# All edge sums beside the sort, marks made on chip, and the search for first edges inside the first node chain of a four-layer graph network

## What is computed

```python
# layer 0: weights summed per node; x scaled, a two-layer MLP, residual, layernorm
geo_sum = segment_sum(edge_weight1 * x[dst], dst); geo_agg = x + geo_sum / segment_sum(edge_weight1, dst)
x = layernorm(x + relu(relu(geo_agg @ W1 + b1) @ W2 + b2))
# layer 1: sum, max and mean of edge_attr_64 per dst node, then an MLP over the node
agg_sum, agg_max = segment_sum(edge_attr_64, dst), segment_max(edge_attr_64, dst)
h = concat([x, agg_sum, agg_max, agg_mean, u]); x = layernorm(x + layernorm(gelu(h @ W1 + b1) @ W2 + b2) + x)
# layer 2: an MLP with a gate on every edge from x[src], x[dst]; mean per SRC node
# layer 3: attention over the edges of each dst node, softmax, sum, batchnorm, gelu
```

## Time and profile before

| | us |
|---|---|
| median of three runs (range) | 6424.94 (6419.04 to 6425.12) |
| profiled execution: its span, first to last instruction | 6445.0 |
| sorted keys are there (end of the split, L545) | 824.4 |
| first load of the node chain (L1013) | 1207.4 |
| last scatter of the node chain ends | 1462 |

### The profile page before, as it was taken

How to read it: one execution, slowest core, us unless ns; L and a number is a source line. 1 busy time by engine, 2 the same in 40 slices (tenths; PEclk the granted TensorE clock), 3 DMA queues, 4 the chain that set the end, 5 groups by cost and what they waited for, 6 DMA issues and landing times. The chain is left out here.

```text
span 6445.0 us, 56951 instructions
## 1 busy us (share of the span) xinstructions
PE 3469.2 (54%) x12150; PEld 1967.8 (31%) x12150; DVE 3716.2 (58%) x4303; ACT 1751.8 (27%) x3305; POOL 3538.9 (55%) x3662
## 2 busy tenths in 40 slices
PE   3565655573443344344444424677666766776772
PEld 2344433341222222222222212333333333333331
DVE  9988955552333333333333343777777777777776
ACT  1233323371111111111111111333333333333331
POOL 5430033326666666666666656666666666666653
PEclk8566667785666666666666655767777677667665
DMA  8756457713333334333333312333333333333331
GB/s 198 208 187 202 150 154 194 132 28 91 102 103 101 103 100 106 99 101 104 106 99 100 104 43 63 86 85 87 85 87 85 86 86 85 86 86 85 88 81 32
DMA packets 994791, 677.97 MB, mean 105 GB/s; under 512 B 645273, under 2 KB 798667, under 8 KB 993734
## 3 DMA queue, kind: packets, MB, share of 16 engines
q1 hardware_dynamic: 718424, 341.42, 21.1%
q0 software_dynamic: 116880, 124.33, 10.4%
q10 hardware_dynamic: 159390, 211.24, 9.7%
HBM read 344.06 MB, written 332.55 MB: 105 GB/s over the span
## 5 line engine op out<-in xcount | busy, mean ns | idle before, releaser
L1655 POOL DMA_INDIRECT got<-tabg,ix x1568 | 1481.5, 945 | 874.7 <-DMA t<-rows 427.9
L1461 POOL DMA_INDIRECT got<-tabg,ix x1568 | 1481.5, 945 | 788.2 <-issue 455.3
L182 PE MATMUL p_out<-ident,run 128*128 128x128 f32 (+1 forms) x3136 | 667.6, 360 | 410.4 <-ACT rows L1519 213.4
L1559 DVE TENSOR_TENSOR_SCAN own<-mk,own,p_first 128x512 f32<-128x512 bf16 x195 | 247.1, 1267 | 1100.0 <-remote 874.4
L182 PEld LDWEIGHTS p_out<-ident,run 128*128 128x128 f32 (+1 forms) x3136 | 547.3, 216 | 733.4 <-issue 599.5
L1481 PE MATMUL p_inter<-hid,W 128*128 128x512 f32 x392 | 313.5, 894 | 806.3 <-issue 676.9
L1790 DVE TENSOR_TENSOR_SCAN top<-p_reset,top,logit 128x512 f32<-128x512 f32 x195 | 249.6, 1280 | 537.3 <-ACT logit L1764 228.7
L168 PE MATMUL p_small<-ident,ea 128*32 128x128 f32 (+1 forms) x784 | 179.6, 376 | 690.7 <-ACT rows L1753 613.8
L1483 PE MATMUL p_gate<-hid,WF 128*128 128x512 f32 x392 | 293.3, 841 | 285.8 <-ACT gate L1513 148.1
L1528 ACT ACTIVATE hid<-pre,B 128x512 f32<-128x512 f32 x196 | 141.2, 720 | 1113.7 <-DVE pre L1575 797.2
L498 DVE TENSOR_TENSOR_SCAN run<-p_mk,run,feat 128x512 f32<-128x512 f32 x302 | 370.5, 1268 | 54.7 <-remote 32.8
(11 more groups left out here) (348 smaller groups left out, 6831.8 us busy)
## 6 DMA issues: line engine op xcount, KB each, us to landing
t<-rows ACTq DMA_DIRECT2D x195, 512.0 KB
first<-start SPq DMA_DIRECT2D x390, 256.0 KB
t<-rows ACTq DMA_DIRECT2D x195, 288.0 KB
got<-tabg,ix POOLq DMA_INDIRECT x3136
start<-zeros SPq DMA_DIRECT2D x100, 500.0 KB
ea<-in_ea_dram SPq DMA_DIRECT2D x390, 128.0 KB
mk<-marks SPq DMA_DIRECT2D x780, 64.0 KB
start<-zeros SPq DMA_DIRECT2D x195, 256.0 KB
```

The costliest lines, as they stand in the source:

```text
L182: mm = nc.tensor.transpose(bank[0:g.p, cc, :], by_place(t, g)[:, :, cc], ident[:, :])
L1461: nc.gpsimd.indirect_dma_start(got[s][0:g.p, cc, h, :], None, tabg, bass.IndirectOffsetOnAxis(ap=ix[0:g.p, g.n, h, cc:cc + 1], axis=0)).th ...
L1655: nc.gpsimd.indirect_dma_start(got[s][0:g.p, cc, h, :], None, tabg, bass.IndirectOffsetOnAxis(ap=ix[0:g.p, g.n, h, cc:cc + 1], axis=0)).th ...
```

## The change

1. `scans_beside` places all 196 groups beside the sort: two in each turn, and 1.154 per other step until the last 32 steps ("quiet"), which have none. The `alone` part and its second set of banks go.
2. The 49 gathers of `t1` move from the chain to POOL beside the quiet steps, once all stores of `t1` have landed; G is allocated outside, cleared in the twelfth turn, and also lends its room to the counts of `Ends`.
3. After the sort SP (no longer POOL) publishes and stores the keys. The marks of the sorted order are made from the keys in SBUF, where one small DMA brings each partition the last key of the one before, and stored by ten DMAs (`mark_rows`). VectorE counts the blocks.
4. `Firsts` replaces `SortedEnds`: the search runs inside the node chain, by units of four columns: `count_rows` in round u + 1, `count_keys` in round u + 5, with POOL's 98 gathers in order rows(n), keys(n - 3). It counts keys less than the node rather than up to the one before, so that a unit has its `first` alone; `last`, `cnt` and `span` are finished at the chain's end.
5. Of the 100 fills 50 stand in the sort, one per three groups, and 50 in the chain, ahead of the index loads; POOL waits for them before its scatters.
6. MC, the carried maximum by node, is made unit by unit in `combine` (one more instruction); XM shares `rows`.

```diff
+            with Stage(nc) as c:
...
+                ends = Ends(nc, sb, ps, sem, c, dst, order[0], nid, rowlast, G)
...
+            node_chain(nc, sb, ps, sem, X, order[0], order[1], srcs, nid, ident, prime, t1, (w2a[D:2 * D, :], w2a[0:D, :]), None, tabg[0], tabo[0], start2, tuple(index_loads(dsts, ix3)),
+                       (wn, w0a, b0a, w0b, b0b, u1, w1a, b1a, w1b, b1b, g1, be1), (G, sums_in, firsts, blank))
...
+    last = len(steps) - QUIET
+    turns = sum(1 for what in steps[:last] if what[0] == "turn")
+    rate = (NG + 1 - 2 * turns) / (last - turns)
     out, n, credit = [], 0, 0.0
-    for what in steps:
-        credit += 0.59
-        if what[0] == "turn" or credit >= 1.0:
-            out.append(n)
-            n, credit = n + 1, max(credit - 1.0, 0.0)
+    for i, what in enumerate(steps):
+        if what[0] == "turn":
+            k = 2
         else:
-            out.append(None)
+            credit += rate
+            k = int(credit)
+            credit -= k
+        if i >= last - 1:
+            k = NG + 1
+        out.append(range(n, min(n + k, NG + 1)))
+        n = out[-1].stop
     return out
...
-                    if len(filled) < 100:
+                    if n % 3 == 0 and len(filled) < FILLED:
                         blank.fill(sp, len(filled), len(filled) + 1)
                         filled.append(n)
                     load(Group(None, n))
-                blank.fill(sp, len(filled), 100)
+                firsts.publish(sp, split)
+                for h in range(2):
+                    sp.wait_ge(split, 2 + h)
+                    t, k = ((si, srcs), (di, dsts))[h]
+                    sp.dma_start(k.rearrange("(p f) o -> p (f o)", p=P), t[:, :]).then_inc(sorted_out, 16)
+                    if h == 0:
+                        with nc.allow_non_contiguous_dma(reason="one key of each row"):
+                            sp.dma_start(before[1:P, :], si[0:P - 1, SF - 1:SF]).then_inc(shifted, 16)
+                firsts.load(sp)
+                for kind in range(2):
+                    sp.wait_ge(marked, 1 + kind)
+                    for part, cols, rows_out in mark_rows(marks[1], kind):
+                        sp.dma_start(rows_out, marks_sb[kind][part, cols]).then_inc(marks_out, 16)
                 sp.wait_ge(indexed, 16 * 4)
-                blank.wait(sp)
+                sp.wait_ge(sorted_out, 32)
+                sp.wait_ge(marks_out, 16 * 2 * 5)
...
-                pool.wait_ge(split, 3)
-                ends_1.publish(pool)
-                for t, k in ((si, srcs), (di, dsts)):
-                    pool.dma_start(k.rearrange("(p f) o -> p (f o)", p=P), t[:, :]).then_inc(sorted_out, 16)
-                ends_1.load(pool)
-                pool.wait_ge(sorted_out, 32)
-                marks_1.load(pool)
-                ends_1.fetch_rows(pool)
-                marks_1.store(pool)
-                ends_1.fetch_keys(pool)
+                pool.wait_ge(sums_cleared, 1)
+                for s in range(2):
+                    pool.wait_ge(stored[s], 16 * ((NG + 2 - s) // 2))
+                for u, (a, k) in enumerate(UNITS):
+                    for j in range(a, a + k):
+                        nc.gpsimd.indirect_dma_start(G[:, j, :], None, t1, bass.IndirectOffsetOnAxis(ap=ends.info["last"][:, j:j + 1], axis=0),
+                                                     bounds_check=E - 1, oob_is_err=False).then_inc(sums_in[u], 16)
...
-                        scan(Group(None, beside[i]))
+                        for n in beside[i]:
+                            scan(Group(None, n))
+                        if turns == CLEAR_TURN:
+                            nc.vector.memset(G[:, :, :], 0.0).then_inc(sums_cleared, 1)
                         dve.wait_ge(back, 4 * turns)
...
-                ends_1.take_rows(nc.vector, ki).then_inc(split, 1)
+                firsts.take_rows(nc.vector, ki).then_inc(split, 1)
                 nc.vector.tensor_scalar(si[:, :], ki, SB, (1 << SB) - 1, ALU.logical_shift_right, ALU.bitwise_and).then_inc(split, 1)
                 nc.vector.tensor_scalar(di[:, :], ki, (1 << SB) - 1, None, ALU.bitwise_and).then_inc(split, 1)
-                for n in range(SORTED, NG + 1):
-                    scan(Group(None, n))
-                    if n == SORTED + 6:
-                        ends_1.count_blocks(dve)
-                    if n == SORTED + 12:
-                        marks_1.compare(dve)
-                    if n == SORTED + 36:
-                        ends_1.count_rows(dve)
-                    if n == SORTED + 66:
-                        ends_1.count_keys(dve)
-                    if n == SORTED + 69:
-                        ends_1.finish(dve)
+                dve.wait_ge(split, 2)
+                mark, reset = marks_sb
+                nc.vector.tensor_tensor(same[:, 1:SF], si[:, 1:SF], si[:, 0:SF - 1], ALU.is_equal).then_inc(compared, 1)
+                dve.wait_ge(shifted, 16)
+                nc.vector.tensor_tensor(same[:, 0:1], si[:, 0:1], before[:, :], ALU.is_equal).then_inc(compared, 1)
+                dve.wait_ge(compared, 3)
+                nc.vector.tensor_copy(mark[:, :], same[:, 0:SF]).then_inc(marked, 1)
+                nc.vector.tensor_scalar(reset[:, :], same[:, 0:SF], -1.0, -NEG, ALU.add, ALU.mult).then_inc(marked, 1)
+                dve.wait_ge(marked, 2)
+                firsts.count_blocks(dve, same[:, :])
...
+    def fetch_rows(self, pool, u):
+        a, k = UNITS[u]
+        pool.wait_ge(self.blocks_counted, 1)
+        for j in range(a, a + k):
+            self.nc.gpsimd.indirect_dma_start(self.rows[:, j, :], None, self.rowlast, bass.IndirectOffsetOnAxis(ap=self.index1[:, j:j + 1], axis=0)).then_inc(self.rows_in[u], 16)
+
+    def fetch_keys(self, pool, u):
+        a, k = UNITS[u]
+        pool.wait_ge(self.rows_counted, u + 1)
+        wait_from(pool, self.found, u - 2)
+        for j in range(a, a + k):
+            self.nc.gpsimd.indirect_dma_start(self.keys[u % 3][:, j - a, :], None, self.key.rearrange("(r s) o -> r (s o)", s=SORTED_KEYS),
+                                              bass.IndirectOffsetOnAxis(ap=self.index2[:, j:j + 1], axis=0)).then_inc(self.keys_in[u], 16)
...
+    def count_rows(self, dve, u):
+        nc, (a, k) = self.nc, UNITS[u]
+        s = slice(a, a + k)
+        dve.wait_ge(self.rows_in[u], 16 * k)
+        node = self.nid[:, s].unsqueeze(2).to_broadcast((P, k, SORTED_ROWS))
+        self.link(dve, nc.vector.tensor_tensor(self.less[:, 0:k, 0:SORTED_ROWS], self.rows[:, s, :], node, ALU.is_lt))
+        self.link(dve, nc.vector.tensor_reduce(self.count1[:, s], self.less[:, 0:k, 0:SORTED_ROWS], AX.X, ALU.add))
+        self.link(dve, nc.vector.scalar_tensor_tensor(out=self.row[:, s], in0=self.block[:, s], scalar=float(SORTED_ROWS), in1=self.count1[:, s],
+                                                      op0=ALU.mult, op1=ALU.add))
+        nc.vector.tensor_copy(self.index2[:, s], self.row[:, s]).then_inc(self.rows_counted, 1)
+
+    def count_keys(self, dve, u):
+        nc, (a, k) = self.nc, UNITS[u]
+        s, keys = slice(a, a + k), self.keys[u % 3][:, 0:k, :]
+        dve.wait_ge(self.keys_in[u], 16 * k)
+        node = self.nid[:, s].unsqueeze(2).to_broadcast((P, k, SORTED_KEYS))
+        nc.vector.tensor_tensor(self.less[:, 0:k, :], keys, node, ALU.is_lt).then_inc(self.v, 1)
+        nc.vector.tensor_tensor(self.upto_it[:, 0:k, :], keys, node, ALU.is_le).then_inc(self.v, 1)
+        self.linked += 2
+        dve.wait_ge(self.v, self.linked)
+        nc.vector.tensor_reduce(self.count1[:, s], self.less[:, 0:k, :], AX.X, ALU.add).then_inc(self.v, 1)
+        nc.vector.tensor_reduce(self.count2[:, s], self.upto_it[:, 0:k, :], AX.X, ALU.add).then_inc(self.v, 1)
...
+                if blank:
+                    blank.fill(sp, FILLED, 100)
...
+                if beside:
+                    for n in range(NU + 3):
+                        if n < NU:
+                            firsts_of.fetch_rows(pool, n)
+                        if n >= 3:
+                            firsts_of.fetch_keys(pool, n - 3)
+                    blank.wait(pool)
...
-                    link(nc.vector.tensor_tensor(G[:, a:a + k, D:2 * D], G[:, a:a + k, D:2 * D], MC[:, a:a + k, :], ALU.max))
+                    link(nc.vector.tensor_tensor(MC[:, 0:k, :], reset[:, a:a + k].unsqueeze(2).to_broadcast((P, k, D)),
+                                                 carry[:, D:2 * D].unsqueeze(1).to_broadcast((P, k, D)), ALU.add))
+                    link(nc.vector.tensor_tensor(G[:, a:a + k, D:2 * D], G[:, a:a + k, D:2 * D], MC[:, 0:k, :], ALU.max))
...
+                        due(t, (ROWS_AT, lambda u: firsts_of.count_rows(dve, u)), (KEYS_AT, lambda u: firsts_of.count_keys(dve, u)))
```

More of the change, by code:

```diff
@@ L401, in sort_and_edge_sums @@
     beside = scans_beside(steps)
-    ticks_of_turns = [beside[i] for i in turns_at]
-    SORTED = max(n for n in beside if n is not None) + 1
-    ALONE = ticks_of_turns[-1] + 1
```

(1 more changed line is left out.)

244 lines of the change are left out of this document (140 added, 104 removed).

## The result

The changed kernel took 6388.3 us (median of four runs, 6380.1 to 6392.8) where the kernel before took 6424.7 beside it: ratio 0.9949, interval 0.9938 to 0.9961, 36 us faster. Forecast were 6380 us. The size is nearly right; the terms behind it are less so. Up to the chain's start two errors of opposite sign, −36 and +75 us, cancelled each other in half. Of the 39 us that were left, 9 came back in the chain and 20 by a quicker chip, in stages whose code is the same.

The account below looks back on a forecast made before the run. VectorE was taken to bound the sort, round trips of ScalarE, TensorE and VectorE the chain. 6445 - 84 (chain's start 1123 against 1207) + 40 (chain) = 6401, less 20 for the median: 6380 us, range 6320 to 6440.

Parts of the forecast that it names:

- The sort without gathers: Sort up to the chain's start: terms 198 + 29 + 22 + 5 + 5 + 22 us added to 822, without the 20 for gathers.
- The busy part: Scans of 80 full groups and a short tail moved beside the sort: 198 us, all on VectorE, added in full.
- The scans in a row: Sort: a scan directly following a scan waits 1.12 us for TensorE to spread its marks; 26 such pairs, 29 us.
- the tail: End of the sort: splitting keys, shifting one key per partition, comparing marks, stores and block counts; 22 us, bounds 17 to 32.
- Turns: Sort's key turns: second scans miss the wait, 12 x 1.8 = 22 us; the last two turns lose their covering scan, 5.
- Gathers beside scans: Three runs of 49 POOL gathers in the sort make turns and double scans suffer: nothing to 60 us, 20 taken.
- The chain: Node chain with the search inside: +20 us for VectorE's counts, +20 for gathers beside the rounds, together +40.
- Rival B: Node chain: the search serialises it, chain +145 us, start-to-end over 339 us, total 6486 us; chance 0.15.
- Later stages: Stages behind the node chain: untouched by the change and of unchanged length.
- the prediction's own signs: Sorted keys 1100 +- 20 us, VectorE over 90% busy from 50 to 1000, chain's first load 1123 +- 25, chain 275 to 320 us.
- C: Sort can't take scans at VectorE's rate: 6.5 us a group in gather stretches, 60 not 20; 6420 us; chance 0.2.
- A: Sort and chain: gathers are harmless when broken up by sort steps and count waits; 6325 us; chance 0.2.

Follow-up runs that it names:

- the spaced kernel: Kernel after, with GpSimd waiting before each pair of its 147 gathers beside the sort for one more VectorE sort step: 6344.0 us on a slow chip, ratio 0.982.
- the spaced kernel before: Kernel before, its two gather runs beside the sort tied to its running sums, two gathers a group: 5554.0 us (0.9991) fast chip, 6393.7 us (0.9885) slow chip.
- the second set: Runs on a slow chip where the kernel before took 6458.6 us; the unchanged kernel after was the control: 6427.4 us, ratio 0.9944.
- the fourth set: Slow chip, before 6422.4 us: kernel after with GpSimd clearing a small tile three times before each of 147 gathers, tied to no engine: 6330.7 us, 0.9861.
- the chain's wait: Kernel after with all three gather runs beside the sort spaced, plus GpSimd's row gathers in the chain waiting for unit n-4's centred result: 6352.4 us, ratio 0.9817.

## Why the prediction was right, and where it was not

**The sort without gathers: 36 us too dear.** Forecast were 198 + 29 + 22 + 5 + 5 + 22 on top of 822, 1103 at the chain's start; with the late releases taken away it is 1066.8 on the slow and 1068 on the fast chip. The busy part was right: VectorE works 745.3 us up to the end of the old sort and 941.3 up to the end of the new, +196. The scans in a row were right (30.6 us, forecast 29), the tail nearly (24.5 for 22). The term that was mis-sized is **"Turns"**, 22 us for second scans that miss the wait and 5 for the last two turns. One turn of the spaced kernel:

```profile
704.70 1.08 ACT L660 ACTIVATE ka<-p_keys 128x512 f32<-128x512 f32 x2 [0.26 <-PE p_keys L632]
...
706.36 2.46 DVE L539 TENSOR_TENSOR_SCAN run<-p_mk,run,feat 128x512 f32<-128x512 f32 x2 [3.04 <-ACT feat L644]
...
708.73 2.34 DVE L575 TENSOR_TENSOR kb<-ka 128x1024 f32<-128x1024 f32 x2
```

The keys are back at 705.78 and the second scan starts 0.6 us later, as in all but one of the twelve turns (0.3 there): 12 x 0.6 = 7 us, where I took 1.8 each, the price at the lower clock, though I had 0.7 for the higher. The last two turns wait 4.4 and 4.5 us without their scan, where they waited 5.2 and 4.2 with it. By groups, first the kernel before up to its last sort step, then the spaced kernel:

```profile
L498 DVE TENSOR_TENSOR_SCAN run<-p_mk,run,feat 128x512 f32<-128x512 f32 x221 | 271.0, 1268 | 11.1 <-PE p_mk L569 6.8 <-ACT feat L606 4.4
L530 DVE TENSOR_TENSOR ka<-kb 128x1024 f32<-128x1024 f32 x116 | 136.2, 1216 | 25.4 <-ACT kb L622 18.9 <-issue 5.8
```

```profile
L539 DVE TENSOR_TENSOR_SCAN run<-p_mk,run,feat 128x512 f32<-128x512 f32 x390 | 476.9, 1264 | 77.9 <-ACT feat L644 46.3 <-PE p_mk L612 24.7 <-issue 7.0
L575 DVE TENSOR_TENSOR ka<-kb 128x1024 f32<-128x1024 f32 x116 | 136.3, 1216 | 9.4 <-ACT kb L660 8.9
L575 DVE TENSOR_TENSOR kb<-ka 128x1024 f32<-128x1024 f32 x116 | 136.2, 1216 | 0.5
```

The old wait ahead of steps (21.9 us in the earlier trace rows, and 25.4) moved ahead of the second scans (4.4 to 46.3 put to feat) and hardly grew. All the idle of VectorE in the sort grew by 26 us (from 74.5 to 100.7), where I had 56.

**Gathers beside scans: 20 us forecast, 82 and about 95 measured.** It is the difference of the chain's starts, spaced and unspaced, on one chip (1148.9 less 1066.8), and 1162.2 less the 1067 of the others on the forecast's own. The mechanism was named, "at 1.00 the other engines all but stop", and the earlier trace rows held its price: two runs of 49 gathers in the alone part cost 101.1 us of waiting. I took 20 since two of three runs beside the sort had gone without harm before, and called 60 the upper bound by the pace of groups. That was the wrong row. Before, VectorE was full of sort steps throughout the first run (90.62 of 91 us) and gathers took 1.54 us. In the kernel after the gathers follow each other at 1.30 us from 93 us on and the first pause (11.3 us) ends at 113; with VectorE idle nothing slows them any more. In the third run they do so from its start, with two turns in it. That a pause feeds itself in this way is my reading of the order of events; no run tests it. Whether a run tips over is not settled by its mean load, and the bound should have been a whole run's length, 64 us, for each of the two runs, as in the earlier trace rows.

**The chain: +40 forecast, +31 to +37 measured** (293.5 and 299.2 us against 262.2). The sum was right. The split, half counts and half gathers, can be read on the fast chip, where no release is late and the chain is 255.8 us against 220.8 in the spaced kernel before, +35. From one y addition to the next the first five rounds there take 54 us against 27 before. GpSimd issues its gathers without a pause of over 0.6 us from the chain's start to 1190 us, eight a round and 10 us of them, and VectorE waits for key rows (12.9 us in the 54). The last seven rounds take 78 against 69, bound by VectorE with its counts. So most of the +35 stands where GpSimd's gathers set the pace, which my sum called no bound ("POOL's floor is lower"), and the counts' 1.9 us a round hold for the last rounds only. Rival B (339 us and more) needed gathers that serialise the chain; three units of depth were enough.

**Later stages: as forecast, unchanged.** The traces of before and after differ there by 40 us in favour of after, but this is two chips: in the second set the unchanged kernel after needs 4977.6 us from edges_3's first gather to the end (1448.1 to 6425.7), where the trace of before has 4975.4 (1469.6 to 6445.0). The slow chips are of two degrees. Where before takes 6422 us, edges_3's gathers span 2245 us and edges_4's 2337 (the fourth set), and the trace of after has 2244 and 2334; where it takes 6459 or 6473 they span 2257 to 2263 and 2354 to 2361, and the trace of before has 2259 and 2355. So the forecast's 20 us between the traced execution and the median were most likely two chips as well, and the median to forecast was of the quicker one.

**Luck.** By the prediction's own signs the sorted keys (1140.2, forecast 1100 +- 20) and the chain's first load (1162.2, forecast 1123 +- 25) are outside their bands, VectorE was far from 90% busy in the pauses, and it was idle in the sort behind late releases, which was to mean "C, or more". Only the chain's length (293.5) and the code behind it are as said. Of the 39 us lost at the chain's start the chain gave 9 back (31 for 40), and the later stages 20: they are 40 us shorter in the trace of after by the chip alone, and the forecast had taken off 20 for what it held to be the difference of trace and median. That the time fell near the forecast is to that extent luck.

**Together**, on alike chips: −58.5 at the chain's start, +37 in the chain, +2 behind it, −19 us between the two traces. The ratio of the medians there says −31. The 12 us between stay open: chips of this degree differ by as much from each other (6459 and 6473 us for before), and there is no trace of before from the second set's chip.

**The rivals.** A said 6325 us if the gathers were harmless when broken up. They are not harmless by themselves. Broken up on purpose they give 0.982 of 6424.7, 6309 us: its price was about right, and its condition was not met. The Trainium skill, "SBUF — State Buffer", section Who interferes with whom, on which it leant, has TensorE and ScalarE wait on nobody. The mild half of that section the traces bear out (a gather of 1.54 us beside sort steps, 1.00 without them); on the other the measurement decides, 82 us of a term that by it would be nothing. Whether ports are behind the late releases at all, no run here shows. C had the right place and sign, a sort that can't take the scans beside gathers, but named the pace of groups as its cause.

**What the change is worth by itself.** Spaced before and spaced after stand at 0.9885 and 0.982, 42 us apart, on slow chips; on the fast chip at 0.9991 and 0.998, 8 us, with intervals that overlap. There, moving the scans wins 30 us at the chain's start and the search gives 35 back to the chain. On the slow chips it wins 72 and gives 33 back. What differs between the kinds of chip is the alone part of the kernel before, which the change removes: spaced, it takes 286 us on the fast chip (812.2 to 1098.3) and 323 on a slow one (815.2 to 1138.6).

The version that beats both kernels is the one with the three runs of gathers spaced (0.982, or 0.9817 with the chain's wait, which adds nothing).

## What to carry to other kernels

A long run of indirect gathers on GpSimd is not free for engines that wait for TensorE, even where it reads nothing of theirs: look at the busy time of all other engines inside each run, and where they fall together while GpSimd goes on at its unhindered pace, spread the gathers between the other engine's steps. Price such a run by its worst row, not by the mean of several. And where traces of two kernels differ in stages whose code is the same, take the difference for the chip's until a control on the same chip says otherwise.

## What the runs showed of the hardware

- While gathers follow each other at 1.25 to 1.3 us for tens of us, engines that wait for TensorE are released late on the slow chips (before: 6422 to 6473 us), up to 45 us behind the recorded end of its work in the sort. On the chip of 5559 us GpSimd never waits for a buffer in the 3136 gathers of the edge loops, at 1.25 us each. At 2.8 to 5.9 us apart, or in pairs, at 2.6 to 2.8 on average, none is late in the sort on a slow chip either; at 1.84 on average (the spaced kernel before) they are 2 to 5 us late, and at 1.32 GpSimd still waits. In the first two runs of the kernel before (1.77 and 1.72 on average, VectorE full of sort steps) none is; at the end of the second run of the kernel after (1.70) some are 4 to 8 us late. Not shown: whether TensorE or its signal is late, what in a gather does it, and what makes the chips differ.
- A low granted clock does not make late releases by itself. It was 0.50 in the first pause (the lower level, 1.2 GHz) and 0.58 over the third run, but also 0.58 from 197 to 281 us in the kernel before, beside 49 gathers and without one. The average over the kernel is 0.67 on slow chips and 0.73 on the fast one.
- The issue of a 1 MB store held SP for 9.89 us, where that of a like one ahead of it had taken 0.41. In the nine other traces of the kernel after and its variants it is 9.2 to 10.5; why is not shown.
